# Attention block on one core: who computes the lower halves of the key differences

## The reference, cut to what matters

```python
q = einsum('bchw,oc->bohw', gn(x), Wq).reshape(b, 8, 64, 2304)   # k and v the same way
attn = softmax(einsum('bhdn,bhdm->bhnm', q, k), axis=-1)
out  = einsum('bhnm,bhdm->bnhd', attn, v)
return x + gamma * out + einsum('bchw,oc->bohw', gn(x), Wsc)
```

## Time and profile before

| | |
|---|---|
| median of 3 runs | 2945.99 us (2945.32 to 2946.71) |
| profiled execution, its own time | 2946.8 us |
| its span, first to last instruction | 2945.1 us |
| granted TensorE clock, mean | 0.998 |
| busy: PE / DVE / ACT / POOL | 98% / 68% / 66% / 93% |

### The profile page before, as it was taken

How to read it: one execution, slowest core, us unless ns; L and a number is a source line. 1 busy time by engine, 2 the same in 40 slices (tenths; PEclk the granted TensorE clock), 3 DMA queues, 4 the chain that set the end, 5 groups by cost and what they waited for, 6 DMA issues and landing times. The chain is left out here.

```text
span 2945.1 us, 153693 instructions
## 1 busy us (share of the span) xinstructions
PE 2891.6 (98%) x71226; PEld 2434.3 (83%) x71226; DVE 2015.9 (68%) x2665; ACT 1949.7 (66%) x3156; POOL 2741.3 (93%) x2043
## 2 busy tenths in 40 slices
PE   6999999999999999999999999999999999999999
PEld 4787888878888888888878888798888888888776
DVE  7777666666677766666677766666666666666663
ACT  4566676776666677677666667767666666666565
POOL 2799999999999999999999999999999999999998
PEclk9999999999999999999999999999999999999999
DMA  3011110110111011010011101101000000000000
GB/s 138 23 51 29 33 38 23 38 34 17 34 38 56 17 31 41 18 54 18 22 30 53 40 22 38 34 28 45 17 24 17 22 18 23 17 23 17 23 16 19
DMA packets 93090, 94.28 MB, mean 32 GB/s; under 512 B 44320, under 2 KB 90400, under 8 KB 92448
## 3 DMA queue, kind: packets, MB, share of 16 engines
q1 hardware_dynamic: 92448, 84.44, 9.5%
HBM read 56.10 MB, written 18.87 MB: 25 GB/s over the span
## 5 line engine op out<-in xcount | busy, mean ns | idle before, releaser
L985 POOL TENSOR_TENSOR PLO<-PE 128x768 f16<-128x768 f32 x1727 | 2502.7, 1470 | 140.6 <-ACT PE L634 115.1
L794 DVE TENSOR_REDUCE mx<-MX 128x2 f32<-128x768 f32 x1728 | 1656.9, 959 | 869.0 <-PE MX L451 849.9
L634 ACT ACTIVATE PE<-SL 128x768 f32<-128x768 f32 x1728 | 1402.3, 811 | 896.5 <-PE SL L477 887.1
L516 PE MATMUL OB<-V,PE 64*128 64x129 f16 x20736 | 1256.3, 218 | 0.8
L516 PEld LDWEIGHTS OB<-V,PE 64*128 64x128 bf16 x20736 | 1004.5, 94 | 220.5 <-DVE Oe L806 3.0
L477 PE MATMUL SL<-QK 64*128 64x384 f16 x10368 | 1167.1, 323 | 11.8 <-ACT PE L634 11.8
L513 PE MATMUL OB<-V,PLO 64*128 64x65 f16 x20736 | 983.8, 191 | 0.0
L386 PE MATMUL PJ<-X,WT 64*128 64x384 f16 (+2 forms) x7675 | 983.1, 301 | 0.0
L513 PEld LDWEIGHTS OB<-V,PLO 64*128 64x128 f16 x20736 | 740.3, 95 | 0.0
L451 PE MATMUL MX<-QK 64*128 64x384 f16 x3456 | 602.3, 323 | 7.6 <-DVE mx L794 6.1
L477 PEld LDWEIGHTS SL<-QK 64*128 64x128 f16 x10368 | 483.2, 94 | 126.4 <-ACT PE L634 17.9
(11 more groups left out here) (109 smaller groups left out, 986.2 us busy)
## 6 DMA issues: line engine op xcount, KB each, us to landing
gx<-x SPq DMA_DIRECT2D x36, 768.0 KB, 4.7
xr<-x SPq DMA_DIRECT2D x96, 192.0 KB, 2.5
out<-xr SPq DMA_DIRECT2D x96, 192.0 KB, 1.9
X<-x SPq DMA_DIRECT2D x6, 768.0 KB, 9.1
CR<-c SPq DMA_TRANSPOSE x96, 2.4
QK<-wk SPq DMA_DIRECT2D x1, 1024.0 KB, 8.9
QK<-wv SPq DMA_DIRECT2D x1, 1024.0 KB, 11.2
QK<-wq SPq DMA_DIRECT2D x1, 1024.0 KB, 11.9
```

The source lines that it names most:

```text
L516: last = pe.matmul(acc, upper, v, start=begin, stop=False, skip_group_check=True)
L634: act.activation(PE32[:, s % PB, :].rearrange("p (h n) -> p h n", h=2), SL[:, :, 0:CH], ACT.Exp, scale=1.0 / SS).then_inc(s_exp, 1)
L794: nc.vector.tensor_reduce(mx3[:, n % 2, :, k], MX[:, :, 0:CH], AX.X, ALU.max).then_inc(s_mxf, 1)
L985: nc.gpsimd.tensor_tensor(PLO[:, s % PB, :], PE32[:, s % PB, :], PE32[:, s % PB, :].bitcast(BF16)[:, 1:4 * CH:2], ALU.subtract).then_inc(s ...
```

## The change

The lower halves that are made in the loop move from GpSimd's queue to VectorE's. They stand in the same steps (four after the projection ended), on VectorE after `top`, `leave` and the reciprocal, and ahead of `bn_stats`. Operands, result and semaphores are the same. The six ahead of the loop stay on GpSimd.

```diff
@@ VectorE's functions
+            def keys_diff_lower(u):
+                g, c = u[1], u[2]
+                dve.wait_ge(s_dh, KCOUNT[u])
+                nc.vector.tensor_tensor(QK[:, g % 2, DL, c * CH:(c + 1) * CH], DF[:, KCOUNT[u] % 2, :],
+                                        QK[:, g % 2, DH, c * CH:(c + 1) * CH], ALU.subtract).then_inc(s_dk, 1)
@@ VectorE's loop
                     if k == LAG and n:
                         invert(n - 1)
+                    done = done_at(s - 4)
+                    if done and done[0] == "k":
+                        keys_diff_lower(done)
                     if stats_part(n, k):
@@ GpSimd's keys_diff_lower (now for the first block alone)
-                g, c = u[1], u[2]
+                c = u[2]
                 pool.wait_ge(s_dh, KCOUNT[u])
-                nc.gpsimd.tensor_tensor(QK[:, g % 2, DL, c * CH:(c + 1) * CH], DF[:, KCOUNT[u] % 2, :],
-                                        QK[:, g % 2, DH, c * CH:(c + 1) * CH], ALU.subtract).then_inc(s_dk, 1)
+                nc.gpsimd.tensor_tensor(QK[:, 0, DL, c * CH:(c + 1) * CH], DF[:, KCOUNT[u] % 2, :],
+                                        QK[:, 0, DH, c * CH:(c + 1) * CH], ALU.subtract).then_inc(s_dk, 1)
@@ GpSimd's loop
                         result_lower(n - 1)
-                    done = done_at(s - 4)
-                    if done and done[0] == "k":
-                        keys_diff_lower(done)
```

## The result

The changed kernel takes 3043.24 us in the median (3041.84 to 3045.11) beside 2946.35 us for the kernel before on the same chip: ratio 1.033, 95% interval 1.0318 to 1.0342, 97 us slower. The forecast was 2996 us, slower, with a range up to 3008. The sign was right; the price, 50 us, was too small by almost half.

The account below looks back on a forecast made before the run. The prediction took TensorE, in its written order, as the bound. Nothing gained from GpSimd's relief, plus 50 us of stalls from VectorE's waits for splits, made 2946.8 + 50 = 2996.8 us, 2996.0 us for the median; range 2945.5 to 3008 us.

Parts of the forecast that it names:

- TensorE sets the time, GpSimd's 93% is hidden, relief is worth 0 to -1.2 us: 90 instructions, 82.7 us, leave GpSimd's queue; TensorE hardly waits for it, so 0 to -1.2 us.
- 0.55 us more on VectorE would hide: Undisturbed key difference fits between VectorE's reductions; only nine places with bn_stats exceed the room, +0.5 us in all.
- Rivals A: VectorE and GpSimd don't disturb each other, or too little to matter: 2946.5 us, not slower; chance 0.25.
- B: Engines share, or a split lets go half way (0.7 us): +10 us, 2956 us; chance 0.12.
- A split in progress holds the key difference to its end: VectorE's two SBUF inputs wait for GpSimd's running split; typical TensorE stalls 0.97 us at step 11, 0.44 at step 16.
- The sum over 90 places, 53 us: Stalls from each place's own starts and ends: 41 us after steps 11, 12 us at chunk ends; 50 taken.
- The chunk ends: The 45 step 16 places: 12 us in all, with 15 of 45 at nothing.
- step 11 of chunk 36: GpSimd works off a backlog; VectorE waits 0.97 us for its second split, TensorE stalls by 0.5 us.
- six of the 45 at about 0.55 us: Six of the 45 step 11 places, priced at about 0.55 us each within the 41 us.
- The walk: The sum carried through all 90 places with their own reductions, exponentials and splits: 53 us, or 41 if splits release at 1.30.
- Rival C, starvation: GpSimd's next ready split goes first in the 36 worst step 11 places: another 51 us, 3047 us; chance 0.05.
- The range: 2945.5 to 3008 us for 8 in 10, taking in A; leaves out C, D (faster) and a small tail.

Follow-up runs that it names:

- e11: Kernel before, with GpSimd's key difference on 4 of 384 columns from the third block on and nothing given to VectorE; 2946.19 us (ratio 1.0).
- e3: Kernel before, with one more VectorE instruction at the 90 places, bn_stats over the same 384 elements of DF into scratch; 2946.89 us (ratio 1.0001).
- e8: Changed kernel, with VectorE's key difference on 128 of 384 columns from the third block on; 3019.2 us (ratio 1.0247).
- e10: Changed kernel, with GpSimd waiting in step 10 of the six chunks with overtaken key differences until its own last split is complete; 3007.18 us (ratio 1.0207).

## Why the prediction was right and wrong

- **TensorE sets the time, GpSimd's 93% is hidden, relief is worth 0 to -1.2 us.** Right: e11, 0 us.
- **0.55 us more on VectorE would hide.** Right for an instruction that nothing holds up: e3, 0.551 us and no change of the time. Rivals A (no disturbance) and B (a short hold, a mean of 0.7 to 1.0 us) fall with the shortest of the 90, 1.465 us.
- **A split in progress holds the key difference to its end.** Right, and the least sure choice of the sum. Step 11 of chunk 73: 1.79 us against 1.38 + 0.55 = 1.93 forecast, the top product behind it 0.81 us late against 0.97. Step 16: 1.47 against 1.58 us, 0.32 against 0.44. The key difference ends 0.41 us after the split, not 0.55. In e8 it ends 0.15 us after, with 256 columns fewer; by these two numbers almost all of the 0.41 us goes with the columns, so its fixed part seems to be over while it waits (an inference). The section of the Trainium skill that the prediction drew on ("SBUF — State Buffer", "Who interferes with whom") is borne out by these 84 places: a VectorE instruction with two SBUF inputs waits for the GpSimd instruction that came first. The other six go against it, since three splits that started after the key difference went ahead of it.
- **The sum over 90 places, 53 us.** Near. e10, where none is overtaken, measures 61 us, a mean of 1.637 us and 61.7 us of waiting of the weight loads, for which the prediction had "near 1.5" and "about 60". In e10 the prices of step 11 add up to 40 us, as forecast (41). The chunk ends cost 20 us instead of 12: single ones cost less than forecast, but at the 15 where the walk had found nothing there is a delay too.
- **The step that failed** is the price of places like step 11 of chunk 36, the "six of the 45 at about 0.55 us". The prediction took that step as an example of GpSimd working off a backlog and priced it at 0.5 us; it is one of the six, and costs 7.2 us. In e10, with the gap, the same place costs 0.5 us. The walk assumed that VectorE is next in turn when the running split ends. Behind a long unbroken row that isn't so: four splits, 5.7 us. The six carry the 36 us between e10 and the kernel after: 6 x (5.7 - 1.6) = 25 us of waiting, and about 11 us is left, in the traces the stretches at half clock in or after each standstill. TensorE is busy some 30 us in the six stretches of the kernel after; an estimate from that is that half clock costs up to 15 us there. That split of the 36 us is worked out, not measured by a run of its own. Which property of a long row lets the splits overtake stays open.
- **Rival C, starvation,** named this mechanism but put it at the 36 worst-phased steps 11, with one more split each, and gave it 0.05 because no row showed such an order. Its time, 3047 us, is near the result by chance: the places and the price of each were different, 36 places of 1.43 us more against six of 6.4 to 7.5 us in all.
- **The range** went to 3008 us. e10's 3007.18 us, the kernel with the starvation removed, lies at its edge; the tail that was left out as small held the result.

The best version remains the kernel before: all that leave more key differences on VectorE are slower, and e11 shows no room on the other side.

## What to carry to other kernels

Before an elementwise instruction is moved from GpSimd to VectorE, look at what it reads. An instruction with one SBUF tensor beside PSUM (L758, 0.54 us), or `bn_stats`, ran freely beside a busy GpSimd; two SBUF tensors or a plain f32 copy waited for it. The price is then not the instruction's length but the wait, and it must be set against the room that VectorE has before the bound engine needs it, here 0.63 + 0.23 = 0.86 us. A GpSimd that is nearly full (93% here) makes long rows: behind such a row without a gap the wait can be several of its instructions, so look for them in the timeline, not at the mean load. One short wait of GpSimd on its own last result, close ahead, opened the row here.

## What the runs showed of the hardware

- VectorE's key difference was held until the running GpSimd instruction ended in 84 places (1.46 to 1.82 us instead of 0.55), and the split behind it was held in turn (1.78 us instead of 1.47 in step 11 of chunk 73; a mean of 1.480 us for all splits instead of 1.470).
- After 23 or more GpSimd instructions without a gap, three or four more ran before VectorE got its turn (5.3 to 6.6 us); after 10 or fewer, none. A gap of 0.08 us one instruction ahead reset this, the same gap 23 ahead didn't.
- A f32 copy of one SBUF tensor was held (mean 1.325 us), `bn_stats` of the same tensor was not (0.551 us).
- Each standstill of TensorE next to an overtaken key difference (4.57 us in the row above, 4.1 to 5.5 us over all runs) came with 3.4 to 6.8 us at a granted clock of 0.50, which began inside the standstill or within 1 us of its end; in e10, where TensorE stood for 1.7 us at most in the loop, there was no such stretch.
